# Second attention of a four-layer model: loops written out for three engines, and one wait of GpSimd moved

## The reference, cut to what matters

```
q = rope(rms_norm(x @ wq))                 # 16 heads of 128, 256 rows a batch
k = concat(rms_norm(ctx @ wk_ctx), rope(rms_norm(x @ wk)))   # 4 key heads, 1601 + 256 keys
v = concat(ctx @ wv_ctx, x @ wv)
scores = q k^T * scale + causal            # each key head serves 4 query heads
out = softmax(scores) v ;  return out @ wo
```

## Time and profile before

| | us |
|---|---|
| median of 3 runs | 2488.07 |
| lowest, highest | 2483.67, 2492.02 |
| the profiled execution, its own time | 2485.85 |
| its span in the profile | 2484.0 |
| mean granted clock of TensorE | 0.982 of full speed |
| second attention (first to last low part) | 563.7 to 1779 |

### The profile page before, as it was taken

The page is one execution under the profiler, slowest core; times in us unless marked ns, Lnnn a source line. Parts: engine busy times, 40 slices in busy tenths (PEclk is TensorE's granted clock), DMA queues, the critical chain, the costliest instruction groups (busy, mean ns, idle before and its releaser), DMA issues.

```text
span 2484.0 us, 53247 instructions
## 1 busy us (share of the span) xinstructions
PE 2348.2 (95%) x19062; PEld 1633.2 (66%) x19123; DVE 1755.4 (71%) x3346; ACT 1740.2 (70%) x3784; POOL 1340.3 (54%) x942
## 2 busy tenths in 40 slices
PE   7989999989999999999999999999899799999997
PEld 4677777757777777777777777777655444444434
DVE  5455768678888887888878888888611567666546
ACT  2234444448887887878878888888611588888897
POOL 1044645436666676666666676666500578778500
PEclk9989999999999999999999999999899999999999
DMA  5122222230001000010000100001310200000100
GB/s 192 63 90 82 85 91 81 79 127 18 1 18 49 18 18 2 18 49 18 18 2 18 49 18 18 1 18 74 132 45 11 70 23 15 24 16 24 54 4 18
DMA packets 42359, 108.67 MB, mean 44 GB/s; under 512 B 5060, under 2 KB 25928, under 8 KB 36936
## 3 DMA queue, kind: packets, MB, share of 16 engines
q1 hardware_dynamic: 40312, 102.28, 12.1%
q0 software_dynamic: 768, 2.10, 0.3%
q10 hardware_dynamic: 1008, 0.79, 0.1%
HBM read 99.78 MB, written 4.98 MB: 42 GB/s over the span
## 4 chain that ended last, share of the span: by engine, by line
PE 61%; DVE 15%; ACT 10%; issue 8%; POOL 4%; DMA 1%; DVEq 0%; another core or an unknown queue 0%; ACTq 0%; SPq 0%; POOLq 0%
PE psum L1674 5%; PE psum L2824 4%; PE psum L2791 3%; ACT l_p L2627 3%; DVE l_plo L1497 3%; PE psum L1722 3%; PE psum L2188 3%; PE psum L1769 3%; PE psum L1703 3%; PE psum L2757 3%; PE psum L1719 2%; PE psum L1720 2%; PE psum L1705 2%; PE psum L1704 2%; PE psum L513 2%
## 5 line engine op out<-in xcount | busy, mean ns | idle before, releaser
L1329 POOL TENSOR_TENSOR xn<-xn,l_p 128x512 f32<-128x512 f32 (+1 forms) x400 | 598.5, 1496 | 251.6 <-DVE l_plo L1497 223.2
L1497 DVE TENSOR_TENSOR l_plo<-l_p,l_phi 128x512 fp32r<-128x512 f32 (+1 forms) x464 | 453.3, 977 | 28.5 <-ACT l_phi L1371 13.0
L2627 ACT ACTIVATE l_p<-psum 128x1024 f32<-128x1024 f32 x416 | 397.7, 1036 | 55.8 <-PE psum L2791 51.2
L1371 ACT ACTIVATE l_phi<-psum 128x512 fp32r<-128x512 f32 (+1 forms) x464 | 277.5, 598 | 138.3 <-PE psum L1722 51.1
L1544 DVE TENSOR_REDUCE l_mx<-psum 128x1 f32<-128x512 f32 (+2 forms) x512 | 303.7, 615 | 52.5 <-PE psum L1769 51.8
L1383 ACT ACTIVATE psum<-l_m 128x512 f32<-128x512 f32 x461 | 283.0, 616 | 7.2
L2602 POOL TENSOR_TENSOR l_rs<-l_ms,half_power 128x32 f32<-128x32 f32 x45 | 244.4, 5432 | 68.8 <-DVE l_ms L2652 58.9
L1372 ACT ACTIVATE l_p<-psum 128x512 f32<-128x512 f32 (+1 forms) x464 | 277.5, 598 | 0.0
L2824 PE MATMUL psum<-l_p,l_vs 64*32 64x256 f32 x6656 | 252.2, 379 | 6.9 <-POOL l_vs L2598 3.1
L1674 PE MATMUL psum<-l_w,l_ctx 128*128 128x256 f32 (+1 forms) x832 | 222.2, 390 | 5.4 <-DVE l_vlo L1537 5.4
L1703 PE MATMUL psum<-l_qThi,l_kThi 128*128 128x512 f32 (+1 forms) x464 | 225.9, 487 | 1.0 <-ACT psum L1383 1.0
(11 more groups left out here) (410 smaller groups left out, 5084.9 us busy)
## 6 DMA issues: line engine op xcount, KB each, us to landing
w_stage<-in_L_w_dram SPq DMA_DIRECT2D x76, 384.0 KB, 3.1
l_w<-in_L_w_qkv_dram SPq DMA_DIRECT2D x16, 1024.0 KB, 4.8
l_ct<-in_ctx_tiles_dram SPq DMA_DIRECT2D x52, 128.0 KB, 2.1
c_T<-in_ctx_T_dram SPq DMA_DIRECT2D x4, 1601.0 KB, 7.8
l_ctx<-in_ctx_T_dram SPq DMA_DIRECT2D x4, 1601.0 KB, 6.8
c_N<-in_ctx_dram SPq DMA_DIRECT2D x4, 1536.0 KB
s_wg<-in_L_gate_dram SPq DMA_DIRECT2D x4, 1024.0 KB, 11.3
s_wu<-in_L_up_dram SPq DMA_DIRECT2D x4, 1024.0 KB, 13.3
```

What stands on the lines that cost most here:

```text
L1329: g_.tensor_tensor(l2_acc[k][0:r, :], first[0:r, :], l2_p[c % 3][0:r, :], ALU.add)\
L1371: act.activation(l2_phi[c % 3][0:r, :], src, ACT.Exp).then_inc(l2_e, 1)
L1497: v.tensor_tensor(l2_plo[c % 3][0:r, :], l2_p[c % 3][0:r, :], l2_phi[c % 3][0:r, :].bitcast(F32), ALU.subtract)\
L2627: act.activation(l3_p[ring(odd, c)][:, :], psum[:, (c % 2) * 2 * BANK:(c % 2 + 1) * 2 * BANK], ACT.Exp, scale=float(D3) ** -0.5).then_inc( ...
```

## The change

`l2_turns` is deleted. DVE, ACT and POOL now run their turns through `l2_turns_written_out`, as PE did. SP's loop over the heads stays. In GpSimd's `sums`, the wait for ACT's full exponential in steps up to 17 (`NPROJ` = 17) becomes the wait for DVE's low part of the same step, which the later steps had already.

```diff
-        def l2_turns(engine, turn, steps=None):
-
-            turn(None, 1, 0)
-            turn(0, 0, 1)
-            looped = TURNS // 2 - 2
-            with engine.Fori(0, looped) as i:
-                if steps:
-                    steps.enter(i, 2 * L2_DVE_STEPS)
-                for s in (1, 0):
-                    g = i * 2 + (2 - s)
-                    turn(g, s, i * 2 + (3 - s))
-            if steps:
-                steps.leave(looped)
-            for g in range(2 * looped + 1, TURNS):
-                turn(g, g % 2, g + 1 if g + 1 < TURNS else None)
@@ l2x_pool, sums
                 if j == 1:
                     need(g_, l2_sum, g * TB + (k - 1))
-                if c > NPROJ:
-                    g_.wait_ge(l2_lo, g * NS + (c + 1))
-                else:
-                    g_.wait_ge(l2_e, g * (3 * NS) + (3 * c + 2))
+                g_.wait_ge(l2_lo, g * NS + (c + 1))
@@ l2x_pool, l2x_scalar, l2x_vector
-            l2_turns(g_, turn)
+            l2_turns_written_out(turn)
-            l2_turns(act, turn)
+            l2_turns_written_out(turn)
-            l2_turns(v, turn, dve_steps)
+            l2_turns_written_out(turn)
-        L2_DVE_STEPS = 2 * TB + 3 + 1 + TB
```

## The result

The changed kernel is slightly slower: median 2499.85 us of 10 runs (2495.51 to 2505.05), against 2486.17 us (2481.97 to 2492.02) before. The ratio is 1.0056, 95% interval 1.0044 to 1.0068, so 13.7 us more, where 19 us less were forecast. The profiled execution has a span of 2495.2 us, 11.2 us more than before.

What follows compares the result with a forecast made beforehand. PE, 95% busy, was taken as the bound, so only its stops or slow running could be gained. Loops -19.7, PE's wait -9 and queue delay +10 made about -19 us: 2468 us, range 2455 to 2480.

Steps and rivals of the forecast that it cites:

- The loops: Five loop jumps of DVE, ACT and POOL in the second attention: removing them saves 19.7 us, stops and slow clock included.
- Waits on constants: Waits on constants in place of registers in the written-out turns: worth nothing, as PE's stream covers it.
- PE's wait at step 4: PE's wait for DVE's low part of step 4 goes: 0.6 us a turn, -9 us over 15 turns.
- First half: Sum of step 1 ends later, moving ACT's exponentials of step 3 by 1.2 us: taken as 0, other end 1.2 a turn.
- Second half: Step 9: the later sum of step 10 delays POOL's root, scaling and next sum: 0.65 us a turn, +10 us.
- The prediction's own sign of being wrong: Wrong if turns are still of two lengths, or all of one length but over 77.5 or under 75.8 us.
- Slower: Delay of step 3's exponentials passes whole to PE through key block 2's copy: 2497 us; chance 0.05, with straight-code stops.
- Only cost: PE's wait at step 4 stays and the second-half cost comes in full: -10 us, 2477 us; chance 0.10.
- only gain: The second-half delay is absorbed, leaving -19.7 - 9 = -29 us: 2458 us; chance 0.27.
- The clock falls anyway: PE's clock still falls at the same or other places, only the stops go: -11 us, 2476 us; chance 0.08.

Runs made afterwards that it cites:

- e1: The changed kernel with GpSimd's old wait, so only the loops are written out: 2465.41 us against 2485.54, ratio 0.9917.
- e8: The kernel before with DVE's turns alone written out; ACT and POOL keep the loop, GpSimd its old wait: 2475.64 us, ratio 0.9953.
- e2: The kernel before with only GpSimd's wait changed; the loops stay: 2521.85 us, ratio 1.0145.
- e9b: The changed kernel with GpSimd's new wait in step 4 alone, other sums up to step 17 waiting as before: 2466.19 us, ratio 0.9921.
- e7: The changed kernel, all new waits kept, with four instead of three buffers for ACT's full exponentials in all turns but the last: 2451.46 us, ratio 0.9860.
- e4: The changed kernel with GpSimd's old wait at the sum of step 10 alone: 2480.70 us against 2487.3, ratio 0.9971.

## Why the prediction was wrong, point by point

*The loops, -19.7 us.* Right: -20.1 us in e1, stops and clock included. One row was misread on the way. The stretch from 1483.78 to 1560.24 does not hold the exit from the loop: turn 12, the last one of the loop, runs from 1498 to 1574 us by ACT's first exponentials. The exit lies in the stretch behind it, which ends with this row of the chain of the kernel before:

```profile
1636.67 1.72 PE psum L1655 x4
```

It is 76.43 us long, so there is no stop at the exit either, and the price stands.

*Waits on constants, nothing.* Nearly: turns of 76.25 us against 76.47, at steps 20 and 24, some 3 us in all. By the misreading above two looped turns were compared. Turn 13 of the kernel before, which is written out, takes 76.30 us, and its step 24 takes 2.06 us as in turn 0, where turns 1 to 12 take 2.19 to 2.20. In e8, with DVE written out, step 24 is 2.20 us still, so its part belongs to the loop of ACT or GpSimd. Step 20 is short with the loops too once the new wait is in (2.97 us in e2). What in the looped code costs this is not shown.

*PE's wait at step 4, -0.6 us a turn.* The size was nearly right (-0.76 us at steps 4 and 5), the reason not. DVE in turn 12 of the changed kernel, beside the earlier trace rows:

```profile
1503.97 1.81 DVE L1503 TENSOR_TENSOR l_m<-ident,l_mx 128x512 fp32r<-128x512 f32 x1
...
1509.94 0.68 DVE L1535 TENSOR_TENSOR l_qb<-l_q,rope_q 128x512 f32<-128x512 f32 x1
1510.65 1.65 DVE L1478 TENSOR_TENSOR l_plo<-l_p,l_phi 128x512 fp32r<-128x512 f32 x1
...
1514.34 2.33 DVE L1537 TENSOR_TENSOR l_qb<-l_qa,l_qb 128x1024 f32<-128x1024 f32 x1
```

The low part of step 4 is as slow as before, 1.65 us. The prediction held that the sum of step 3 would be done by then; it starts at 1509.29 beside the products of the queries, takes 2.45 us and runs beside this low part too. What got faster are the two products ahead of the low part (L1535: 0.68 us, 1.77 us before as L1554; the other 0.67 us, 1.57 before): here the sum is held, and not they. In exchange, two other operations got slower: L1503 takes 1.81 us (0.72 before, as L1522) and L1537 2.33 us (1.22 before, as L1556).

The Trainium skill ("SBUF — State Buffer", section "SBUF: two separate sides") calls the shared port pair an exclusive lock, held for a whole instruction. The trace agrees with what the prediction made of it, that the loss would change its place: DVE's busy time fell by only 4.3 us in 1755.4. But PE's wait at step 4 went all the same, since the operations that are slow now do not hold up what PE waits for there.

*And it was not kept.* The prediction took 0.6 us of PE's wait as 0.6 us of the turn. In e9b it is given back by step 11, most of it six steps later. The kernel before already stood close to a second limit there, POOL's root, scaling and sum 7, which ACT's exponentials of step 10 wait for.

*First half: the sum of step 1, nothing.* Right for PE: the exponentials of step 3 waited 1.00 us and PE's steps 2, 3 and 6 are unchanged. But I looked only at who waits for this sum, not at what stands behind it on POOL: the root of the queries (1505.19) ended, and sum 2 started, about 1.4 us later. The sums of steps 3 to 6 each start right behind their own low part.

*Second half: the step that failed.* The forecast of about nothing for GpSimd's wait, -9 and +10 us, failed at its second term, the queue behind the held sums. "In step 9 POOL first does the sum of step 10, then the root (L1350) and the scaling (L1352), then the sum of step 11" was priced, and the same place at step 5 (sum 6, root, scaling, sum 7) was not, although the front part of the text names all four. It cost 1.45 us at step 10. (The 0.24 us at step 7 come another way: e7, where ACT hangs on no sum, has 0.28 us there.) This was in reach: the kernel before had ACT's exponentials of step 10 start within 0.2 us of the end of sum 7. *The one that was priced*, 0.65 us, cost 1.16 us, at steps 13 and 14 and not at the last projection; ACT's exponentials of step 14 waited 1.94 us for POOL, since the sum of step 11, meeting DVE, took 2.1 us, where 1.3 us or a little more was taken. e4 and e7 show the two places: with the old wait at sum 10 the second loss goes and the first stays, and with a fourth buffer the first goes wholly and of the second 0.27 us is left.

*The sum.* -0.76 + 0.24 + 1.45 + 1.16 - 0.24 (steps 20 and 24) = +1.85 us a turn, 28 us over 15 turns, where I had about 0. With -19.7 us it makes +8 us; in the profiled executions the attention became 10.1 us longer from the first low part to that of turn 15. Some 0.9 us of the difference lies in turn 0, where step 10 took 6.90 us, 3.53 before. Turn 15, which prepares no other and which the prediction left out, took 2.7 us more as well, 55.7 us against 53.1 (53.0 in e1, so it is the wait). The rest of the kernel was 1.6 us shorter, which makes the 11.2 us of the spans. The prediction's own sign of being wrong was met: all turns of one length, but over 77.5 us.

*The rivals.* "Slower" gave 2497 us, close to the 2499.85 measured, and needed 1.9 us a turn, which was right. Its path, from the exponentials of step 3 to the bank of block 2, was not, so that its number came close is luck. "Only cost" took PE's wait at step 4 to stay, and it went; "only gain" took the second half to be absorbed, and it was not. "The clock falls anyway" fell as a price: none of the turns begins with a fall. One short fall, 3.4 us from 586.91 on, lies in turn 0, right behind a stop of PE of 2.22 us for the query transposes of step 10:

```profile
587.06 1.09 PE L1762 MATMUL psum<-ident,l_q 128*128 128x128 f32 x4 [2.22 <-DVE l_qTlo L1546]
```

## What to carry to other kernels

When a wait is added to an engine that works through a queue, walk that queue to its next idle time and price every item behind the wait, at each place of the turn, with the buffers that it returns; here it was not the sum that waits that hurt, but the root, the scaling and the next sum behind it. A bottleneck engine's wait is worth its length only if the next wait behind it has slack, which one can read from how close the next releases lie. And if one engine's lateness reaches another only through a rotation of buffers, one more buffer may turn a loss into a gain. Here 2499.85 us became 2451.46 us with the same waits.

## What I had not expected of the hardware

An operation of DVE with two inputs in SBUF took up to 1.1 us longer beside one sum of GpSimd (1.29 us alone), at each of three lengths: 128x128 went from 0.28 to 1.36 us, 128x512 from 0.72 to 1.81 us, 128x1024 from 1.22 to 2.33 us.

And a short stop of PE was often followed by 6.8 us at the lower clock (0.50 granted, 1.2 GHz in place of 2.4). In the kernel before, PE stood still for 2.0 to 2.2 us at each of the five jumps, and the clock fell behind the first four. In e2, with stops of the same length, it fell behind two of five. In e8, where about the same loss of a jump is spread over waits of 0.45, 0.29 and 1.67 us, it fell behind none. In e2 a fall made the turn 1.6 us longer (82.8 us against 81.2).
